# Last stores of the count stage issued from the attention stage, and three pieces of work moved with them

## What is computed

```python
ft = einsum('nhd,ed->nhe', hh, W_fc)              # hh: x as 1250 x 12 x 64
a1, a2 = einsum('nhd,hd->nh', ft, attn_l), einsum('nhd,hd->nh', ft, attn_r)
e = leaky_relu(a1[src] + a2[dst], 0.2)
m = segment_max(e, dst)
ee = exp(e - m[dst])
alpha = ee / segment_sum(ee, dst)[dst]
agg = segment_sum(alpha[:, :, None] * ft[src], dst)
x = layernorm(x + relu(res + agg))
```

## Time and profile before

| | before |
|---|---|
| median of 3 runs | 2479.14 us |
| the profiled execution's own time | 2480.09 us |
| its span in the trace | 2478.3 us |
| first window of the count stage on PE | at 44.12 us |
| last instruction of the count stage on ACT ends | at 371.00 us |
| last issue of the count stage on SP ends | at 389.62 us |
| first instruction of the attention stage on SP | at 390.12 us |
| first unit of head 0 on DVE (L774) | at 426.15 us |
| first weights of head 0 on POOL (L647) | at 432.63 us |
| last instruction of the attention stage (POOL, L654) ends | at 814.1 us |

### The profile page before, as it was taken

How to read it: one execution, slowest core, us unless ns; L and a number is a source line. 1 busy time by engine, 2 the same in 40 slices (tenths; PEclk the granted TensorE clock), 3 DMA queues, 4 the chain that set the end, 5 groups by cost and what they waited for, 6 DMA issues and landing times.

```text
span 2478.3 us, 29974 instructions
## 1 busy us (share of the span) xinstructions
PE 2173.8 (88%) x10953; PEld 1837.3 (74%) x10954; DVE 1228.3 (50%) x1882; ACT 780.9 (32%) x1062; POOL 451.2 (18%) x378
## 2 busy tenths in 40 slices
PE   3998761888888389999999999999999899999997
PEld 1555440333333179999999999999999899999997
DVE  7887656999995452233333342232333342344335
ACT  0133332888886231121221231121221231212212
POOL 0000001899999200000000000000000000000000
PEclk9999885999999589999999999999999999999999
DMA  0133332211110523333423423333323423335332
GB/s 17 42 86 88 89 91 59 89 32 32 32 32 16 159 90 88 99 90 105 121 83 114 113 71 89 97 106 110 117 77 108 123 66 103 121 102 139 100 99 78
DMA packets 138639, 215.04 MB, mean 87 GB/s; under 512 B 87580, under 2 KB 87818, under 8 KB 138513
## 3 DMA queue, kind: packets, MB, share of 16 engines
q1 hardware_dynamic: 99179, 147.28, 21.1%
q0 software_dynamic: 39344, 66.16, 9.3%
HBM read 182.38 MB, written 30.62 MB: 86 GB/s over the span
## 4 chain that ended last, share of the span: by engine, by line
PE 58%; DMA 5%; DVE 2%; ACT 2%; issue 0%; SPq 0%; ACTq 0%; DVEq 0%
PE banks L1101 30%; PE banks L1073 27%; DMA w_raw<-in_L_gnn_w_root_dram 3%; DVE w_lo L1342 1%; ACT w_hi L1221 1%; DMA s_x<-x_tiles 1%; PE banks L1136 1%; DMA emb_raw<-in_L_gnn_w_rel_dram 0%; PE banks L1110 0%; PE banks L1123 0%; PE banks L1154 0%; DVE h_lo L1373 0%; ACT accT L1249 0%; DVE tail_stats L1392 0%; DVE back L1390 0%
## 5 line engine op out<-in xcount | busy, mean ns | idle before, releaser
L1073 PE MATMUL banks<-ct_in,h_hi 125*128 125x416 f32 (+1 forms) x1710 | 604.5, 353 | 0.6 <-ACT accT L1206 0.6
L1073 PE MATMUL banks<-ct_in,h_lo 125*128 125x416 f32 (+1 forms) x1710 | 603.2, 353 | 0.0
L1101 PE MATMUL banks<-g_hi,w_hi 128*128 128x416 f32 (+1 forms) x1440 | 518.4, 360 | 21.6 <-DVE g_lo L1364 21.5
L1101 PE MATMUL banks<-g_lo,w_hi 128*128 128x416 f32 (+1 forms) x1440 | 513.7, 357 | 0.0
L1101 PE MATMUL banks<-g_hi,w_lo 128*128 128x416 f32 (+1 forms) x1440 | 513.4, 357 | 0.0
L1342 DVE TENSOR_TENSOR w_lo<-w_raw,w_hi 128x768 fp32r<-128x768 f32 (+1 forms) x228 | 227.9, 1000 | 468.2 <-ACT w_hi L1221 468.2
L1221 ACT CAST w_hi<-w_raw 128x768 fp32r<-128x768 f32 (+1 forms) x228 | 197.8, 868 | 449.8 <-PE banks L1101 354.6
L1073 PEld LDWEIGHTS banks<-ct_in,h_lo 125*128 125x128 f32 x1710 | 323.7, 189 | 4.4
L1073 PEld LDWEIGHTS banks<-ct_in,h_hi 125*128 125x128 f32 x1710 | 322.5, 189 | 4.1 <-ACT accT L1206 0.8
L1237 ACT CAST g_hi<-gs 128x416 fp32r<-128x416 f32 (+3 forms) x180 | 97.5, 542 | 702.7 <-DVE gs L1352 702.7
L849 PE MATMUL head_sums<-pw,x 125*65 125x512 f32 x720 | 273.0, 524 | 51.5 <-POOL pw L647 35.2
(11 more groups left out here) (189 smaller groups left out, 1538.5 us busy)
## 6 DMA issues: line engine op xcount, KB each, us to landing
w_raw<-in_L_gnn_w_rel_dram SPq DMA_DIRECT2D x117, 384.0 KB, 3.3
ct_in<-s_ct POOLq DMA_DIRECT2D x18, 2031.2 KB, 28.1
w_raw<-in_L_gnn_w_rel_dram SPq DMA_DIRECT2D x54, 448.0 KB, 3.9
ct_in<-s_ct POOLq DMA_DIRECT2D x9, 2041.0 KB, 28.4
s_ct<-ct_stage SPq DMA_DIRECT2D x30, 610.4 KB
w_raw<-in_L_gnn_w_root_dram SPq DMA_DIRECT2D x39, 384.0 KB, 3.2
w_raw<-in_L_gnn_w_root_dram SPq DMA_DIRECT2D x18, 448.0 KB, 5.8
low_spread<-s_low SPq DMA_DIRECT2D x12, 610.4 KB
```

Of the source, the lines that this page charges most:

```text
L1073: ins = nc.tensor.matmul(pb[0:rows, PA, 0:s.w], a, b, start=j == 0, stop=j == len(pairs) - 1)
L1101: ins = nc.tensor.matmul(pb[:, m, 0:s.w], a, b, start=s.first and j == 0, stop=s.last and j == len(parts) - 1)
```

## The change

Four edits.

1. **Stores.** In the count stage SP issues of the last two tiles only the first store of tile 8. The other two of tile 8 with its degree row, and all four of tile 9, are issued by SP in the attention stage, behind the loads of `wfc` and of head 0's x. There the barrier no longer waits for them; what needs them waits for `stored`. ACT widens the csum tiles in the order 6, 7, 8, 9, then 0, 1, 2 (behind `stored[0]`), then `keep_low(0)` and 3, 4, 5 (behind `stored[1]`). The unit u takes buffer (u + 3) % 5 of `y`, so that units 0 to 4 write where the already widened tiles of `csum16` lay. `bend_low(u)` waits for 2u + 2 widened tiles in place of all ten for unit 0, `weights(u)` for its own tile.
2. **Ranges.** DVE makes the ranges behind the 11th of the 20 `oh_rem` instructions, not behind the 20th.
3. **Head 0's a1** is spread into `r1` instead of `a1`, so that head 1's first two matmuls needn't wait for head 0's maxima; the third does, since it shares a PSUM bank. `spread_r1(0)` now waits for head 0's maxima.
4. **Degrees.** `degrees` runs behind the fourth unit of the last head, and its DMAs (the read of the degree rows, ten stores of the reciprocals) near the end of SP's list. The one number that a later stage asks for (`many`) is no longer brought over by a PE transpose but by a DMA of 30 numbers, and read at the end (`most`).

```diff
@@ count_matrices, SP: the last two tiles
-            tile(NT // 2 - 1, 0)
-            tile(NT // 2 - 1, 1, False)
+            tile(NT // 2 - 1, 0, kept=2)
+            tile(NT // 2 - 1, 1, more=False, kept=3)
             sp.wait_ge(rows_out, 32 * NT)
@@ count_matrices, DVE
             for i in range(0, NRUN, REM_R):
                 nc.vector.tensor_tensor(oh_rem[:, i:i + REM_R, 0:T, :], ...)
+                if i == NRUN // 2:
+                    ranges()
...
@@ attention, SP
             load_x(0)
-            for b in range(2):
-                sp.wait_ge(stored[b], 16 * (R + 1) * (NT // 2))
-            sp.wait_ge(proj_out, 16 * NT)
-            sp.dma_start(part, dram["deg"]...).then_inc(deg_in, 16)
+            for b, kept in ((0, 2), (1, 3)):
+                g = NT - 2 + b
+                for r in range(R - kept, R):
+                    sp.dma_start(dram["ct"][r].rearrange("(s p) d -> p s d", p=T)[:, :, g * T:(g + 1) * T],
+                                 stage[0:T, b, r]).then_inc(stored[b], 16)
+                sp.dma_start(dram["deg"][g:g + 1, :], stage[T:T + 1, b]...).then_inc(stored[b], 16)
             ... nt ...
             load_x(1)
             spread_low(0)
-            sp.wait_ge(inv_ready, 1)
-            for t in range(NT):
-                sp.dma_start(dram["inv"][:, t * T:(t + 1) * T], deg[t * R:(t + 1) * R, :]).then_inc(inv_out, 16)
             spread_low(1)
@@ attention, ACT
-            for b in range(2):
-                act.wait_ge(stored[b], 16 * (R + 1) * (NT // 2))
             act.wait_ge(proj_out, 16 * NT)
-            for t in range(NT):
+            for t in WIDENED:
+                if t == 0:
+                    act.wait_ge(stored[0], 16 * (R + 1) * (NT // 2))
+                if t == 3:
+                    act.wait_ge(stored[1], 16 * (R + 1) * (NT // 2))
+                    keep_low(0)
                 nc.scalar.copy(csum[:, t], csum16[:, t]).then_inc(widened, 1)
-            keep_low(0)
             keep_low(1)
@@ attention, DVE
                 best(NT + t)
                 if t == NT // 2:
-                    degrees()
+                    weight_turned()
...
+                    if h == H - 1 and s == 3:
+                        degrees()
@@ attention, PE
             def spread(h):
-                if h:
+                to = a1 if h else r1
+                if h >= 2:
                     pe.wait_ge(maxed, h * NT)
-                for i, (o, w) in enumerate(SPANS):
+                for i, (o, w) in enumerate(SPANS if h else R1_SPANS):
+                    if h == 1 and i == 2:
+                        pe.wait_ge(maxed, NT)
```

More of the change, by code:

```diff
@@ L154, in _, with tile @@
                 sp.dma_start(tabf[:], rng[:, 2:3]).then_inc(tab_in, 16)
-            def tile(tt, b, more=True):
+            def tile(tt, b, more=True, kept=0):
                 g = tt * 2 + b
@@ L165, in tile @@
                     sp.dma_start(a_rows[m * H:(m + 1) * H, bass.ds(g * T, T)], splitrow[:, m]).then_inc(rows_out, 16)
-                tile_staged(sp, tt, b)
-                for r in range(R):
+                if kept < R:
+                    tile_staged(sp, tt, b)
+                for r in range(R - kept):
                     sp.dma_start(dram["ct"][r].rearrange("(s p) (u c d) -> p s u c d", p=T, c=2, d=T)[:, :, bass.ds(tt, 1), b].rearrange(
                         "p s u d -> p s (u d)"), stage[0:T, b, r]).then_inc(stored[b], 16)
-                sp.dma_start(dram["deg"][bass.ds(g, 1), :],
-                             stage[T:T + 1, b].rearrange("a r s d -> a (r s d)")).then_inc(stored[b], 16)
+                if not kept:
+                    sp.dma_start(dram["deg"][bass.ds(g, 1), :],
+                                 stage[T:T + 1, b].rearrange("a r s d -> a (r s d)")).then_inc(stored[b], 16)
             with sp.Fori(0, NT // 2 - 1) as tt:
@@ L497 @@
 YS = 5
+Y_AT = [(u + 3) % YS for u in range(NU)]
+WIDENED = [6, 7, 8, 9, 0, 1, 2, 3, 4, 5]
 GONE = 1e25
@@ L501, with attention @@
 R1_SPANS = [(286, 512), (798, N - 798), (0, 286)]
-def attention(nc, io, dram, x, res, share, oT, cols, csum, csum16, nbr, y, stored, proj_out, rows_out, node, ident):
+def attention(nc, io, dram, stage, x, res, share, oT, cols, csum, csum16, nbr, y, stored, proj_out, rows_out, node, ident):
     a1_high, a1_low, a2_col, a_rows = cols
@@ L597, in _ @@
             sp.wait_ge(maxed, NU)
+            for b in range(2):
+                sp.wait_ge(stored[b], 16 * (R + 1) * (NT // 2))
+            sp.dma_start(part, dram["deg"].rearrange("t (r s d) -> (t r) s d", r=R, s=NT)).then_inc(deg_in, 16)
             sp.dma_start(kinds_at.bitcast(I32), io["node_type_3"].rearrange("(a n) -> a n", a=1).to_broadcast([64, N])).then_inc(small_in, 16)
@@ L600, in _ @@
             sp.dma_start(emb, io["L1_gnn_node_emb"]).then_inc(small_in, 16)
+            sp.wait_ge(inv_ready, 1)
+            for t in range(NT):
+                sp.dma_start(dram["inv"][:, t * T:(t + 1) * T], deg[t * R:(t + 1) * R, :]).then_inc(inv_out, 16)
+            sp.wait_ge(most_in, 1)
+            with nc.allow_non_contiguous_dma(reason="30 numbers"):
+                sp.dma_start(top_row, top_col[:]).then_inc(top_in, 16)
             sp.wait_ge(inv_out, 16 * NT)
@@ L802, in _ @@
             emb_columns()
+            most()
             divide(H - 2)
@@ L1493, in build @@
         h_lo = t("h_lo", [T, NT, D1], F32R)
-        attention(nc, io, dram, x, res, share, oT, (a1_high, a1_low, a2_col, a_rows), csum, csum16, nbr, y, stored, proj_out, rows_out, (hot, hot_rows, emb_cols, many), ident)
+        attention(nc, io, dram, under[0], x, res, share, oT, (a1_high, a1_low, a2_col, a_rows), csum, csum16, nbr, y, stored, proj_out, rows_out, (hot, hot_rows, emb_cols, many), ident)
         ct0 = t("ct_in0", [T, NT, WIDE], F32R)
```

99 lines of the change are left out of this document (51 added, 48 removed).

## The result

The changed kernel took 2485.24 us (median of 17 runs, 2478.52 to 2493.55) beside 2480.29 us for the kernel before (17 runs on the same chip, 2477.77 to 2487.14). The ratio is 1.0021, interval 1.0013 to 1.0029: some 5 us longer, with 3 to 7 us inside the interval. The forecast was 2481.6, range 2475.5 to 2487.5. The profiled execution took 2481.92 with a span of 2480.1 (2478.3 before), so it is one of the shorter ones. The ratio is right on the edge of the 0.2% that were taken for no change.

What follows compares the result with a forecast made beforehand. Different limits by stretch: SP's table DMA, the barrier waiting for SP's issues, then DVE ahead of unit 0. Terms -2.0 + 3.45 + 1.1 = +2.55; from 2479.14, + 2.5 gives 2481.6 us, range 2475.5 to 2487.5.

Steps and rivals of the forecast that it cites:

- no gap: Last head, POOL: the forecast would be wrong if no gap of about 1 us showed there.
- Ranges, -2.0: Ahead of the count stage's first window: earlier ranges hide SP's table DMA, cast at 41.1, -2.0 us for all behind.
- The barrier, 369.5: End of count stage: without the stores the next stage opens at 371.5, less 2.0, 18.6 us earlier, if unit 0 follows.
- The stores' path, 58.1 from opening to unit 0: Attention stage start: five stores, then the low write and `low_spread` in SP's queue, set unit 0 at 429.6, +3.45 us.
- the passing write: Rival, SP's queue: the low write passes head 1's x, unit 0 at 425.8, 3.8 less, 2477.8 us; chance 0.12.
- DVE's own path, 402.8 in the clock of before: Ahead of unit 0: DVE ready at 402.8; as the deciding rival 2454.8 us, chance 0.10 for all or part.
- Degrees, +1.1: Last head: degrees behind unit 3 delay unit 4 and leave POOL a gap, +1.1 us, bounds 0 to 3.84.
- 0 if it has more lead: Last head: lower bound on the degrees' price, 0 us if there is more lead than counted.
- Casts and buffers, 0: Before unit 0: widening done by 421, so new waits of `weights` and the order of `y` cost nothing; at most 3.5.
- The rival of late landings: Between stores and unit 0: transfers land late, +3.6, 2485.2 us; chance 0.18 together with larger prices of the degrees.
- the rival of the 2.0 us given back: Count stage regains its old pace and the ranges' gain is lost: 2483.6 us; no chance of its own.
- us for us: Attention stage: a later unit 0 taken as an equally later end of the stage.

Runs made afterwards that it cites:

- ranges last: Changed kernel with the ranges made behind the 20th `oh_rem` again, as before: 2486.67 us, ratio 1.0023 to the kernel before.
- the repetition: The changed kernel run and profiled once more, unaltered: 2486.47 us, ratio 1.0022 to the kernel before.
- low rows first: Changed kernel with `nt` and head 1's x issued behind head 0's low-row DMAs, not ahead: 2480.59 us, ratio 1.0003 to the kernel before.
- Two of tile 8 stay: Changed kernel with one more of tile 8's stores, two in all, kept in the count stage: 2478.18 us, ratio 0.9995 to the kernel before.
- one of tile 9 ahead: Changed kernel, tile 8's stores and tile 9's first ahead of the barrier, low rows before x, their copy before ACT's store wait: 2457.61 us, ratio 0.9919.
- before + degrees: Kernel before with only the degrees moved into the last head, with their DMAs: 2474.97 us, ratio 0.9984 to the kernel before.
- this table: The dropped table of the kernel before, the changed kernel, its repeat and the follow-up kernels: median, ratio, and one profiled execution each.
- the changed form: The changed kernel, its repeat and its edited variants, without the kernel before and that kernel with degrees alone: ratios 0.9919 to 1.0023.

## Why the prediction was right

The mechanism was right where the time is made: the moved stores and the low write behind them set unit 0, and the barrier's earlier opening was not usable. The forecast size was half of what came out: +2.5, and some 5 measured. Two terms were off, the barrier's opening and the last head, where the forecast had itself named "no gap" as a sign of being wrong.

- *Ranges, -2.0:* cast at 41.11 (forecast 41.1), first window at 42.18 (42.1). Kept to unit 0, as "ranges last" shows.
- *The barrier, 369.5:* it opened at 372.43, 2.9 late. This is the mis-sized term. The barrier does wait for the engines alone, as forecast, but ACT's last mask ended at 372.17, not 369.0. Just ahead of the last window PE stood 1.60 us, before 0.36, and then the last window took 2.20 us at a lower clock, before 1.48 (next fences). These two make 2.0 of the 3.2 us by which ACT ended late; the rest came earlier in the stage and on the way from the last window to the mask. The late end came again in the repetition (371.79) and in "ranges last" (373.80, from a start 2.0 later). But "low rows first" has the same gap, its last window at full clock, and ACT's end at 369.89: the gap alone does not make the 2.9. In the others with the ranges early ACT ended between 369.3 and 370.3. The kernel before with the degrees alone ended at 372.17 too, against 371.00, so an opening is uncertain by a microsecond.
- *The stores' path, 58.1 from opening to unit 0:* it took 430.35 - 372.43 = 57.9. Terms: `stored[1]` at 417.1, 44.7 behind the opening (forecast 45.5). Two misses cancel in it: the last packets of the stores and degree rows end 43.6 behind the opening (forecast 43.1), and ACT is released 1.1 behind them, not 2.4. The 2.4 was misread from the dip in the earlier trace rows: in the kernel before those packets end at 395.45, 0.75 ahead of ACT. The low write's return is at 423.25, 50.8 behind the opening (forecast 50.6); `low_spread` issued at 423.55, unit 0 6.8 later (7.2 forecast). "Two of tile 8 stay" shows the price of a store, 7.5, and "low rows first" the price of the line, 4.9 where 4.0 were expected. The forecast's own 3.8 for the passing write is too high by its terms: with `low_spread` behind x at 421.1, 5.0 of bytes and 1.0 to the landing, unit 0 would be near 427.2, 2.4 less.
- *DVE's own path, 402.8 in the clock of before:* "one of tile 9 ahead" shows it as the next bound.
- *Degrees, +1.1:* 0. POOL had no gap, in the changed kernel nor in "before + degrees". My bound "0 if it has more lead" was the case. I had counted one unit of lead; but DVE waited for POOL just before (1.20 us at 770.75, 0.59 at 775.47), so it was ahead by all the five buffers of `y`. The earlier trace rows had such a wait already, 0.84 us for POOL at 772.19.
- *Casts and buffers, 0:* nothing waits for them at unit 0; POOL's first weights come 5.52 behind it (forecast 5.7, before 6.48).

The rival of late landings named 2485.2 us, and 2485.24 came out. That is chance: it wants a path of 61.7 us from opening to unit 0, and 57.9 were measured.

Three smaller slips stand in the forecast: 762.61 + 7 x 2.6 is 780.8, which makes the degrees +0.95 and not +1.1; the passing write and another 2 us give 2475.8 as the low end of the range, not 2475.5; and the rival of the 2.0 us given back has no chance of its own.

By these terms the sum is -2.0 + 2.9 + 3.45 - 0.2 = +4.2 at unit 0, and 4.08 at the stage's end. The profiled span shows just 1.8 of it: from the next stage's first load to the end it was 1663.9 before and 1661.6 after, while the nine other executions of this table lie between 1661.4 and 1666.5, with no order by edit. The medians' difference of 4.95 (3 to 7 by the ratio) agrees with the 4.1. The median was 3.6 above the forecast of 2481.6: 2.9 for the late opening, -1.1 for the degrees, and 1.15 because the kernel before took that much more on this chip than in the runs the forecast started from (2480.29 against 2479.14). The other 0.7 lies inside the interval.

That the sum closes so well is luck in part. By the ratios, the nine timings of the changed form stand 0.3 us below to 4.5 above what the shift of unit 0 alone would make of the kernel before (1.0 in the changed kernel, 1.9 on average); in "before + degrees" it is 0.4. That would fit a price of the long heads of some 1 to 2 us, which the forecast, with a later unit 0 as a later end "us for us", does not hold. It is an estimate from one profile of each, and not shown by an experiment.

The last window (PE's timeline) and the stretch of the late opening in the changed kernel, columns as above:

```profile
360.21 0.19 PE L410 MATMUL win<-zero_a 125*128 125x1 bf16 x2 [1.60 <-issue]
360.59 2.20 PE L426 MATMUL win<-oh_key,oh_rem 125*128 125x375 bf16 x8 [0.19 <-issue]
...
359.00:361.00 2.00, 0.60 (x5) 0.45 (x6) 0.94 (x3) 0.51 (x2) 0.00 (x0) 1.00 0.34 94
361.00:363.00 2.00, 2.00 (x9) 1.19 (x8) 0.00 (x0) 0.14 (x1) 0.00 (x0) 0.54 0.12 46
363.00:365.00 2.00, 1.91 (x10) 1.72 (x9) 0.00 (x0) 1.90 (x4) 0.00 (x0) 0.60 0.00 0
```

And in the kernel before:

```profile
360.33 1.48 PE L421 MATMUL win<-oh_key,oh_rem 125*128 125x375 bf16 x8 [0.19 <-issue]
...
359.00:361.00 2.00, 1.45 (x11) 0.85 (x10) 1.64 (x4) 0.85 (x2) 0.00 (x0) 1.00 0.34 82
361.00:363.00 2.00, 2.00 (x16) 1.60 (x14) 0.00 (x0) 1.12 (x3) 0.00 (x0) 1.00 0.38 83
```

PEclk is 0.54 from 361 to 363, behind the gap (the lower level is 1.2 of 2.4 GHz, 0.50), and PE does 9 matmuls in 2 us where before it did 16. In "low rows first" the last window, behind the same gap, still ran at full clock:

```profile
359.02 1.49 PE L426 MATMUL win<-oh_key,oh_rem 125*128 125x375 bf16 x8 [0.22 <-issue]
```

Left open: the 1.60 us gap. It is there in the four profiles of kernels that keep only one of tile 8's stores ahead of the barrier (1.56 to 1.62), 1.28 with two, and 0.36 to 0.54 with all three. It goes with the number of stores; by what path PE is held was not found.

## To carry to other kernels

When a barrier waits for stores, moving them behind it takes no byte away: ask first what will wait for the last of them, and what is issued behind them in the same queue. A small transfer that the next stage needs goes ahead of the bulk loads, and the copy that feeds it ahead of the wait for the stores; only then does the earlier opening count (18 us here, against a loss of 5; tile 8's stores went back and the two orders were changed for it). And of a group of stores, leave those ahead of the barrier that the queue has room and time for: each one moved behind it cost unit 0 7.5 us here, while those left ahead held the opening by 2.9 us at most.

## What the runs showed that I had not expected

- An issue of a 610 KB store takes SP 0.3 to 0.4 us while the queue has room (336.25: 0.41, with DMA at work beside it) and up to 7.8 us on a full one (the three at 389.48 take 15.72 together). The degree row behind them is 14.6 KB and takes as long, 7.19. SP's time is then the queue's, and a barrier that needs SP waits for transfers that nobody waits for.
- A write of 15 KB came back in 1.36 us with nothing ahead, 4.74 behind stores and 5.77 behind two loads.
- The heads' 30 us run on so small a lead of PE over POOL that a head in which the granted clock falls to its lower level takes 32 to 33 us. Two executions of the same kernel differ by 5 us in this, as much as the whole effect of the change.
